# First edge layer: last 392 columns in their own bank and computed first; attention terms of a head spread one tile sooner

## What is computed

```python
fs = (x @ Ws + bs).reshape(-1, H, D)
fd = (x @ Wd + bd).reshape(-1, H, D)
e = jax.nn.leaky_relu(fs[src] + fd[dst], 0.2)
logits = jnp.einsum('ehd,hd->eh', e, attn)
```

## Time and profile before

| | |
|---|---|
| median of 3 runs | 3059.64 us (3055.92 to 3059.67) |
| the profiled execution's own time | 3062.38 us |
| its span, first to last instruction | 3060.6 us |
| mean granted TensorE clock | 0.905 |
| PE busy | 2528.6 us (83%) |
| DVE busy | 2157.8 us (71%) |
| ACT busy | 1362.9 us (45%) |
| POOL busy | 759.1 us (25%) |

### The profile page before, as it was taken

The page is one execution under the profiler, slowest core; times in us unless marked ns, Lnnn a source line. Parts: engine busy times, 40 slices in busy tenths (PEclk is TensorE's granted clock), DMA queues, the critical chain, the costliest instruction groups (busy, mean ns, idle before and its releaser), DMA issues.

```text
span 3060.6 us, 41464 instructions
## 1 busy us (share of the span) xinstructions
PE 2528.6 (83%) x12635; PEld 2024.1 (66%) x12636; DVE 2157.8 (71%) x4356; ACT 1362.9 (45%) x2651; POOL 759.1 (25%) x939
## 2 busy tenths in 40 slices
PE   5979999876999955689999999777987798888574
PEld 2536666575699934678999999736744454766573
DVE  7988888886576646788878788657764336675454
ACT  0026666562377721566656566407411100633452
POOL 4858888800066622000000000100000000001002
PEclk8979999987999985899999999888998899987797
DMA  9701100062033411777656666520000201001786
GB/s 316 246 23 34 34 31 30 21 169 84 21 45 55 40 22 35 252 254 253 226 186 218 227 224 228 172 115 1 30 31 17 67 0 47 17 1 47 269 302 210
DMA packets 83611, 351.82 MB, mean 115 GB/s; under 512 B 26984, under 2 KB 27421, under 8 KB 75950
## 3 DMA queue, kind: packets, MB, share of 16 engines
q1 hardware_dynamic: 56772, 300.70, 30.9%
q0 software_dynamic: 26656, 48.90, 5.0%
HBM read 292.28 MB, written 57.23 MB: 114 GB/s over the span
## 4 chain that ended last, share of the span: by engine, by line
PE 59%; DVE 19%; DMA 7%; POOL 6%; issue 5%; ACT 4%; SPq 0%; POOLq 0%; ACTq 0%; DVEq 0%
PE PS L853 14%; PE PS L943 10%; PE PS L990 7%; PE PS L1087 6%; PE PS L1089 3%; DMA C<-in_L_ffn_expert_w 3%; POOL logits L731 2%; PE PS L976 2%; PE PS L1106 2%; PE PS L1108 2%; PE PS L1107 2%; DVE w1s L2226 1%; DVE w3s L2319 1%; PE PS L1177 1%; DVE w2s L2231 1%
## 5 line engine op out<-in xcount | busy, mean ns | idle before, releaser
L853 PE MATMUL PS<-large_rows,turned 125*128 x1448 | 528.1, 367 | 39.5 <-issue 18.3
L853 PE MATMUL PS<-small_rows,turned 125*128 x1448 | 492.1, 343 | 0.0
L731 POOL DMA_INDIRECT logits<-lgr,key x362 | 361.8, 1000 | 248.4 <-DVE lgr L1833 175.7
L943 PE MATMUL PS<-WB,XT 128*125 128x384 f32 (+1 forms) x1120 | 389.6, 508 | 0.0
L1087 PE MATMUL PS<-urowsT,w1s 128*128 128x384 f32 (+2 forms) x1164 | 356.3, 371 | 31.5 <-DVE F L2239 19.8
L853 PEld LDWEIGHTS PS<-large_rows,turned 125*128 125x128 f32 x1448 | 272.7, 188 | 89.0 <-issue 76.7
L943 PEld LDWEIGHTS PS<-WB,XT 128*125 128x125 f32 x1120 | 213.1, 193 | 160.9 <-issue 36.3
L990 PE MATMUL PS<-F,PT 125*125 125x96 f32 (+3 forms) x1500 | 288.1, 344 | 19.2 <-ACT PT L1415 8.2
L1089 PE MATMUL PS<-urowsT,w1s 128*128 128x192 f32 (+2 forms) x1164 | 298.6, 257 | 0.0
L853 PEld LDWEIGHTS PS<-small_rows,turned 125*128 125x128 f32 x1448 | 272.3, 188 | 8.1
L990 PEld LDWEIGHTS PS<-F,PT 125*125 125x125 f32 x1500 | 226.7, 199 | 60.9 <-issue 17.9
(11 more groups left out here) (367 smaller groups left out, 5210.9 us busy)
## 6 DMA issues: line engine op xcount, KB each, us to landing
XN<-in_L_ffn_w SPq DMA_DIRECT2D x98, 769.0 KB, 4.4
PB<-in_L_ffn_w SPq DMA_DIRECT2D x97, 768.0 KB, 5.6
WB<-node_ids SPq DMA_DIRECT2D x44, 512.0 KB
C<-in_L_ffn_expert_w SPq DMA_DIRECT2D x17, 1152.0 KB, 5.4
NEG<-in_L_ffn_expert_w SPq DMA_DIRECT2D x17, 1152.0 KB, 5.4
logits<-NEG SPq DMA_DIRECT2D x8, 1367.2 KB
WB<-logits SPq DMA_DIRECT2D x5, 2187.5 KB
slot_rows<-NEG POOLq DMA_DIRECT2D x13, 768.0 KB, 56.5
```

The costliest lines, as they stand in the source:

```text
L731: pool.indirect_dma_start(out=table, out_offset=bass.IndirectOffsetOnAxis(ap=key[:, i:i + 1], axis=0), in_=lgr[:, i % EU, 0:HEADS[g]["h"]] ...
L853: mm = pe.matmul(out, ohT[i % 3][:, (1 - side) * P:(2 - side) * P], part[side][:, bass.ds(c, 1), a:b].rearrange("p o n -> p (o n)"), start ...
L943: mm = pe.matmul(PS[0:R, 4 + g % 4, 0:hw], XT[:, k, t * R:(t + 1) * R], w[:, k, half * hw:(half + 1) * hw], start=(k == 0), stop=(k == kc ...
```

## The change

There are two parts.

**First edge layer.** `zA` becomes the first 392 columns of bank 7 and takes the last 392 columns of the node rows. `zB` becomes columns 128 to 511 of bank 6, beside the tally, and takes the first 384 columns. On PE the matmuls to `zA` come first in a tile, start afresh and wait for `s_wa`; then come the waits for the one-hots and for `s_zr`, the tally, and the matmuls to `zB`, which only add. On ACT the clear is now that of `zB` (384 columns) for the same tile i. It stands right behind the tail copy of tile i and waits for `s_mul`, the read of `zB` of tile i - 1. Both steps of the one-hots follow it. On DVE `weigh_end` and `weigh_start` take 384 columns each.

**Heads.** `broadcast` of the next head stands one unit sooner, ahead of the `turn` of the third tile of a head.

```diff
-        zA = PS[:, 6, P:P + GW - 512]
-        zB = PS[:, 7, 0:512]
+        zA = PS[:, 7, 0:GW - HB]
+        zB = PS[:, 6, P:P + HB]
...
-                    wait(pe, s_zr, i)
+                    wait(pe, s_wa, i)
+                    pe.wait_ge(s_tt, i + 1)
+                    node_rows(zA, i, cd, cs, HB, GW).then_inc(s_za, 1)
+                    if i % 4 == 1 and i // 4 + 1 < EW // 4:
+                        then = blocks_of(i // 4 + 1)
                     pe.wait_ge(s_oh, i + 1)
                     if i % 2:
                         pe.wait_ge(s_odd, i // 2 + 1)
+                    wait(pe, s_zr, i)
                     pe.matmul(tallied[:, bass.ds((cd * T + cs) * P, P)], oht[i % 8], ohs[i % 8], start=False,
                               stop=i == ES - 1, skip_group_check=True).then_inc(s_ohu, 1)
-                    pe.wait_ge(s_tt, i + 1)
-                    node_rows(zA, i, cd, cs, 512, GW, first=False).then_inc(s_za, 1)
-                    if i % 4 == 1 and i // 4 + 1 < EW // 4:
-                        then = blocks_of(i // 4 + 1)
-                    wait(pe, s_mul, i)
-                    node_rows(zB, i, cd, cs, 0, 512).then_inc(s_zp, 1)
+                    node_rows(zB, i, cd, cs, 0, HB, first=False).then_inc(s_zp, 1)
...
-                    if kind == "gat" and place(s)[1] == T - 2 and place(s)[0] + 1 < h:
+                    if kind == "gat" and place(s)[1] == T - 3 and place(s)[0] + 1 < h:
                         broadcast(place(s)[0] + 1)
...
                     act.copy(tails[:, i % EU, :], tail).then_inc(s_tc, 1)
                     if g == 0:
+                        if i:
+                            act.wait_ge(s_mul, i)
+                            act.copy(zB, NEG[:, 0, 0:HB]).then_inc(s_zr, 1)
                         if i + 2 < ES:
                             turned_gap(i + 2)
-                        if i + 1 < ES:
-                            act.wait_ge(s_wa, i + 1)
-                            act.copy(zA, NEG[:, 0, 0:GW - 512]).then_inc(s_zr, 1)
-                        if i + 2 < ES:
                             turned_onehot(i + 2)
```

More of the change, by code:

```diff
@@ L1365, in edge_parts @@
                         act.wait_ge(s_lg, -(-ES // 4) * g + i // 4 - 2)
-                    tail = zA[:, D - 512:GW - 512] if g == 0 else zw[i % 4][:, 1, HB:GW - HB]
+                    tail = zA[:, D - HB:GW - HB] if g == 0 else zw[i % 4][:, 1, HB:GW - HB]
                     act.copy(tails[:, i % EU, :], tail).then_inc(s_tc, 1)
                     if g == 0:
+                        if i:
+                            act.wait_ge(s_mul, i)
+                            act.copy(zB, NEG[:, 0, 0:HB]).then_inc(s_zr, 1)
                         if i + 2 < ES:
                             turned_gap(i + 2)
-                        if i + 1 < ES:
-                            act.wait_ge(s_wa, i + 1)
-                            act.copy(zA, NEG[:, 0, 0:GW - 512]).then_inc(s_zr, 1)
-                        if i + 2 < ES:
                             turned_onehot(i + 2)
@@ L1840, in weigh_end @@
                     wait(dve, s_hd, i - 1)
-                    dve.scalar_tensor_tensor(out=prod[i % 2][:, 512:D], in0=zA[:, 0:D - 512], scalar=0.0,
-                                             in1=PB[:, 2 * D + 512:3 * D], op0=ALU.max, op1=ALU.mult).then_inc(s_wa, 1)
+                    dve.scalar_tensor_tensor(out=prod[i % 2][:, HB:D], in0=zA[:, 0:HB], scalar=0.0,
+                                             in1=PB[:, 2 * D + HB:3 * D], op0=ALU.max, op1=ALU.mult).then_inc(s_wa, 1)
                 def weigh_start(i):
                     dve.wait_ge(s_zp, i + 1)
-                    dve.scalar_tensor_tensor(out=prod[i % 2][:, 0:512], in0=zB, scalar=0.0,
-                                             in1=PB[:, 2 * D:2 * D + 512], op0=ALU.max, op1=ALU.mult).then_inc(s_mul, 1)
+                    dve.scalar_tensor_tensor(out=prod[i % 2][:, 0:HB], in0=zB, scalar=0.0,
+                                             in1=PB[:, 2 * D:2 * D + HB], op0=ALU.max, op1=ALU.mult).then_inc(s_mul, 1)
                 def head_sums(i):
```

## The result

| | before | after |
|---|---|---|
| median | 3059.65 us (4 runs, 3055.92 to 3064.74) | 3116.58 us (4 runs, 3115.51 to 3118.55) |
| ratio | | 1.0186, 95% interval 1.0168 to 1.0203 |
| profiled execution, its span | 3062.38 us, 3060.6 us | 3116.87 us, 3115.1 us |
| mean granted TensorE clock | 0.905 | 0.911 |

The change makes the kernel 57 us slower. The lines move by one or two: `weigh_end` is now L1840, `weigh_start` L1845, `head_sums` L1850, the clear L1371, the tally L885, `finish` L1832, `terms` L1396 and the evacuation L1950.

A forecast was written before the change was run, and what follows sets the result against it. Bound: in the first edge layer a closed ring of waits over DVE, ACT and PE, 2.251 us a tile. 3062.4 + 68.6 + 0.4 - 31 = 3100.4, less 2.7 gives a median of 3097.7 us, range 3070 to 3124.

The forecast's parts named there:

- The ring: First edge layer: `zA` matmuls, tail copy, clear, tally, `zB` matmuls in series; 2.63 us a tile against 2.251, 68.6 us lost.
- seven starts: First edge layer, PE: seven gaps to the last of eight matmuls, 0.176 each plus 0.085 behind a pause, 1.32 us.
- The mis-sized term: First edge layer: hand-over from the end of ACT's clear to PE's tally, 0.22 us, taken from the profile before.
- the high end of 2.74: First edge layer: the tile's length if the clear doesn't overlap the tail copy (+0.11), 88 us lost.
- The clear: First edge layer, ACT: clearing 384 columns takes 0.485 us by the rows, against 506 ns by the skill page.
- What was costed at nothing: First edge layer: new waits for `s_mul` and `s_wa`, DVE's two products, register loads, POOL's scatters; no cost.
- The heads: Attention with 8 and 4 heads: the sooner broadcast removes ACT's stall at head changes; 31 us gained (16 to 35).
- DVE's ring of 10.50: Attention with 8 heads: DVE evacuates a unit every 2.10 us, 10.50 for five, claimed as what is late next.
- the term of 10.85: Attention with 8 heads: time a head after the change, 10.50 plus 0.35 of PE's extra 1.32; 16.6 us gained.
- A faster kernel: Rival, first edge layer: overlaps keep the tile below 2.42 us, so the change pays; median 2987, chance 0.07.
- The clock didn't fall: Denies a rival, first edge layer: PE's 0.8 us idle a tile lowers the clock, 63 us more, 3161; chance 0.06.
- The broadcast did what it says: Denies a rival, heads: PE's extra 1.32 us delays units as much as ACT's stall did; about 3129, chance 0.05.

The follow-up runs named there:

- the control: The changed kernel with PE's loads of block numbers moved behind the matmuls to `zB`; 3147.34 us, ratio 1.0268.
- a kernel with four further edits: The changed kernel with clear ahead of tail copy, PE's clear wait first, `zB` 304 and `zA` 472 columns, `head_sums` behind its own tile's products; 3044.19 us.
- a fifth: The kernel with 304 and 472 columns, with PE's loads of block numbers moved behind the matmuls to `zB`; 3023.88 us, ratio 0.9870.

## Why the prediction was right, and where its sizes were off

**The ring** was named rightly, in the order of its members. Each term against the timeline of the changed kernel:

| term | predicted | measured |
|---|---|---|
| tally to first matmul | 0.17 | 0.13 |
| seven starts | 1.32 | 1.33 |
| last start to tail copy | 0.38 | 0.38 |
| tail copy to clear | 0.06 | 0.06 |
| clear | 0.485 | 0.489 |
| end of clear to tally | 0.22 | 0.32 |
| sum | 2.63 | 2.71 |

**The mis-sized term** is the last one. The prediction took it from the old hand-over and didn't see that the diff also moves the wait for `s_zr` behind the other waits of PE. The run with the old order gives 0.21 and 2.613 a tile, 0.02 from the 2.63 of the sum. So of the 84.2 us, (692.6 - 203.2) - (672.3 - 201.9) = 19 are the order of the waits and 65 the ring, for which 68.6 stood in the sum. That the whole, 2.719 a tile, still lies under the high end of 2.74 is luck: that end allowed 0.11 for a clear that doesn't overlap the tail copy, which didn't happen, and the hand-over grew by about as much.

**The clear.** The rows gave 0.485 and it took 0.489. The estimate from the Trainium skill, ScalarE: Activation LUTs (What ACT_TABLE_LOAD costs), was 506 ns; it is 17 ns too long here, as it was 22 ns too long for 264 columns. Its figure is for an ACTIVATE, and these rows are of COPY.

**What was costed at nothing** cost nothing. The wait for `s_mul` ahead of the clear never showed: the clear has no idle time before it. `weigh_start` waits 0.39 for PE and that hurts nobody, for DVE is idle 22 us in 100. The register loads were said to lie in PE's pause, and they did; the control shows that this cover was worth some 30 us (3147.34 against 3116.58). DVE's two products kept their sum (0.558 twice), but the one-hot of odd tiles (L1855) grew from 0.249 to 0.454 us on average, so DVE's work of a tile is 2.13, not 2.02. It stands off the ring and cost nothing here.

**The heads.** 31 us were expected and 29.3 measured. A head gives 13.22 - 10.99 = 2.23 with 8 heads (2.37 expected) and 14.90 - 12.30 = 2.60 with 4 (2.4 expected). With 4 heads the mechanism was right: what was late next was PE, busy for the whole 12.30, where 12.17 was summed, and the stall of 1.97 that is left costs nothing. But 14.90 was the mean of a window in which the clock had fallen (15.74) and one in which it hadn't (14.06), and the prediction took it for the first kind.

With 8 heads two statements were wrong. The stall doesn't go, it shrinks from 2.71 to 0.65; and what is late next isn't DVE's ring of 10.50. ACT works without any other wait in the window of 10.99: 10.34 busy and 0.65 of stall. In the kernel before it was the same, 10.51 busy and 2.70 of stall of 13.25. So the term of 10.85 (10.50 and 0.35 that gets through) came near 10.99 by luck. The prediction also left the clock out with 8 heads, where it was 0.87; that cost little.

**The rivals.** A faster kernel would have needed a ring below 2.42; it came only in a kernel with four further edits (2.311), and a ring below the 2.251 of before only with a fifth (2.195). The clock didn't fall: 1.00 in the window from 400 to 500, and from 203 to 692 us as a whole, with PE idle for 0.91 us ahead of every tally. The case of the Trainium skill, TensorE: Matmul & The Clock Gate (A second HAM failure mode: psum-queue depth-cycling), pauses between groups that make the clock swing, isn't seen in this phase. The broadcast did what it says.

**The total** came 19 us above the forecast of 3097.7: the edge layer lost 16 more than summed, by the profiled executions, and the heads gave 2 less.

**Open.** What in PE's waits costs the 0.10 us. Why a one-hot of DVE beside a scatter is long. Why the clock fell behind some pauses at a head change and not behind others. Whether the tally could run ahead of the wait for the clear wasn't tried: its last 128 columns lie in the bank of `zB`, and nothing would then order them against DVE's read of that bank.

## What to carry to other kernels

When a step is swapped from one buffer to another, write down the new ring of waits with every engine's queue in it, and sum it from the hand-overs in the trace. Here a clear that had run beside half of PE's matmuls came in series with all of them. Read the diff for the order of the waits on one engine as well as for the waits: put the wait that will end last first, and those that are over behind it, if the instruction stands in the ring. And when a ring is made shorter, look for what the old pause had covered, such as register loads on every fourth turn.

## What the runs showed of the hardware

- The order of waits on different semaphores ahead of a matmul of PE matters. With the one that ends last in front of one or two that are over, the matmul starts 0.22 us after the end of the ACT copy; with it behind them, 0.32 to 0.33. Written twice behind two others, it is 0.43.
- PE idle for 0.91 us in each 2.72 us, over 490 us, left the granted clock at 1.00. In the attention with 8 heads, with PE idle for 0.44 us ahead of each broadcast, two heads of five had 0.86 and took 12.21 instead of 11.02.
- PE's loads of block numbers into registers hold back its next matmul by some 0.5 us where nothing covers them (0.71 from the last start to the tally with them, 0.22 without; 3.28 instead of 2.72 for the tile in the control).
- A one-hot of DVE (128x128, f16 to bf16) took 0.25 us in the kernel before. In the kernel with 304 columns it took 0.46 to 0.75 where it started 0.27 us or more behind the start of a scatter of POOL (1.03 us long), and 74 of these 75 ended with the scatter.
